# Moving the vectors' pair products from VectorE to GpSimd, and turning them by transposes that add in PSUM

## The chip, the cores and the metric

The kernel runs on one core of a Trainium2 chip. Such a core has five engines with queues of their own: TensorE (matrix products, called PE in the profile, its weight loads PEld), VectorE (DVE), ScalarE (ACT), GpSimd (POOL) and SyncE (SP), which here only starts transfers. They meet through semaphores. The metric is the time of one execution on the device in microseconds (us); lower is better.

## The reference, cut to what matters

A graph network of four layers over 6250 nodes and 206250 edges; after each layer comes `x = layernorm(x + layer(x))`. A node row has 160 numbers: 64 scalars and 32 vectors of 3 components. In the last two layers (L2 and L3) the edges' messages are summed into their node, and then the node is updated:

```python
# a0, a1: the summed messages' scalars (n, 64) and vectors (n, 32, 3); xs, xv: the node's own
u0 = jnp.einsum('nu,nv,uvw->nw', xs, a0, Wu_ss) * INV64 \
   + jnp.einsum('nui,nvi,uvw->nw', xv, a1, Wu_vv) * (INV_SQRT3 * INV32)
u1 = jnp.einsum('nu,nvi,uvw->nwi', xs, a1, Wu_sv) * INV_SQRT2048 \
   + jnp.einsum('nui,nv,uvw->nwi', xv, a0, Wu_vs) * INV_SQRT2048
u0 = u0 + xs @ Lu_s * INV8
u1 = u1 + jnp.einsum('nui,uw->nwi', xv, Lu_v) * INV_SQRT32
return node_features + jnp.concatenate([u0, u1.reshape(n, 96)], axis=-1)
```

The change concerns the second term of `u0`: for every node the 32 x 32 products of the node's vectors with the message vectors, added over the three components, and then contracted with `Wu_vv`.

## The kernel before

Each layer has an edge part (`e0` to `e3`) and a node part (`n1` to `n4`). The parts follow one another and their tiles bear the part's letter. The change lies in `nodes_update`, which is run twice, as `n3` and as `n4`. It works on 50 blocks of 128 nodes, one node to a partition. Every engine has its own instruction list, written out by hand, with a function `step(s)` that is run for every block; the lists keep their order, and semaphores alone hold them together. In one step an engine works on up to three blocks: `s` (its row is being loaded and its message sums turned), `b = s.back(1)` (its update is computed) and `p = s.back(2)` (its layer norm is finished).

- SyncE loads block `s`'s row `row`, once the update step of the block that used that buffer has been done (`upd_set`), and stores the finished block.
- GpSimd copies the message sums of block `s` out of the big accumulator into `own` (L1932), and takes the inverse root in the layer norm of block `p` (`inverse_root`, L771).
- TensorE turns rows and sums (`front`), multiplies the sums by the message weights (`messages`, which gives `agg`), and for block `b` turns the pair products in ten halves of 4 x 128 columns (`turn_half`): halves 0 to 7 are the scalars' products `ss`, halves 8 and 9 the vectors' products `vv`. ScalarE copies every turned half to SBUF, and `contract_half` contracts it with the weights `WQ`. The scalars are turned by `pe.transpose`. For the vectors, three ordinary matmuls by the identity add the three components in PSUM; an ordinary matmul of fp32 leaves two records in the trace, a transpose one. `columns` (four per block) make the matrices of which VectorE forms `u1`. Half 8 comes after `front(s)`; then contraction 7, columns 2 and 3, `messages(s)`, half 9 and contractions 8 and 9.
- VectorE forms `ss` in four pieces of 1024 and `vv` in one of 3072 elements a partition (`pair_products`, L1954 and L1959), then finishes block `p` (`finish`: the update step L1968, layer norm, L1976 as the last), and then forms the `u1` products of block `b` (`vector_products`: twice two multiplications L1988 and a sum L1993).

The piece of `ss` with number 2 or 3 reuses the buffer of number 0 or 1 and waits until TensorE has turned it. There is one `vv` buffer. `linked` counts the four linked steps of one `finish`; its last count is the memset at L1976, behind the normalisation.

Of the kernel before, what the change touches and what calls it, by code (L numbers as in the profile page):

```python
# [8 lines left out]
ALU = mybir.AluOpType  # L9
# [3 lines left out]
P = 128  # L13
# [8 lines left out]
CS, CV = 64, 32  # L22
D = CS + 3 * CV
# [66 lines left out]
def run_steps(eng, step, lag, unroll, number, held=(), peel=1):  # L90


    turns = number // unroll
    assert turns * unroll == number and lag <= unroll
    for i in range(peel):
        for j in range(unroll):
            step(Tile(i, j, unroll, number))
    with eng.Fori(peel, turns) as i:  # L98
        registers = {(a, c): eng.snap(eng.to_reg(i * a + c)) for a, c in held} or None
        for j in range(unroll):  # L100
            step(Tile(i, j, unroll, number, 0, registers))
    for j in range(lag):
        step(Tile(turns, j, unroll, number))
# [10 lines left out]
def bcast(ap, shape):  # L114
    return ap.to_broadcast(list(shape))
# [648 lines left out]
def layernorm(dve, chain, y, stats, out, squares, roots, item, nth, each):  # L764
    moments(dve, chain, y, stats, squares)
    return normalise(dve, y, stats, out, roots, item, nth, each)


def inverse_root(pool, at, power, squares, roots, item, nth, each):
    pool.wait_ge(squares, item.count(nth, each))  # L770
    pool.tensor_tensor(at, at, power, ALU.pow).then_inc(roots, 1)  # L771
# [945 lines left out]
def nodes_update(nc, g, A, name, mats, x, acc, x_out, scales, message_scales):  # L1717
# [11 lines left out]
    HALVES = 10  # L1729
    CHUNKS = 5  # L1730
    REST = CAT - 4 * P
    with Phase(nc, name) as ph:
        two = range(2)

        def pair(name, shape):
            return [ph.sb(f"{name}{k}", shape) for k in two]
        WZ, WQ, WL, WM = ph.sb("WZ", [P, 2 * CH]), ph.sb("WQ", [P, 40, CS]), ph.sb("WL", [P, 2, D]), ph.sb("WM", [P, CHUNKS, D])
        row, agg, a0T, rowT, accT, lastT = pair("row", [P, 2 * P]), pair("agg", [P, D]), pair("a0T", [P, P]), pair("rowT", [P, 2 * P]), pair("accT", [P, 4 * P]), pair("lastT", [REST, P])
        own, ss = pair("own", [P, CAT]), pair("ss", [P, SQ])
        vv = ph.sb("vv", [P, 3 * CV * CV])  # L1740
# [12 lines left out]
        row_in, stored = (ph.sems_of(n, 2) for n in ("row_in", "stored"))  # L1753

        with nc.Block() as block:
# [21 lines left out]
            def _(pe):  # L1777
# [28 lines left out]
                def turn_half(b, h):  # L1806
                    if h < 8:
                        pe.wait_ge(ss_set, b.count(h // 2 + 1, 4))
                    else:
                        pe.wait_ge(vv_set, b.count(1))  # L1810
                    if h >= 2 or b.reuses(1):
                        pe.wait_ge(half_sb, b.count(h - 1, HALVES))
                    for c in range(4):
                        to = ps_s[h % 2][:, c * P:(c + 1) * P]
                        if h < 8:
                            at = (4 * (h % 2) + c) * P
                            ins = pe.transpose(to, ss[h // 2 % 2][:, at:at + P], g.ident[:, :])  # L1817
                        else:
                            at = (4 * (h - 8) + c) * P
                            for k in range(3):  # L1820
                                ins = pe.matmul(to, vv[:, k * CV * CV + at:k * CV * CV + at + P], g.ident[:, :], start=k == 0, stop=k == 2)
                    ins.then_inc(half_ps, 1)

                def contract_half(b, h):
# [99 lines left out]
            @block.gpsimd  # L1924
            def _(pool):
                pool.wait_ge(blank, 1)

                def step(s):
                    if s.exists():
                        if s.reuses(2):  # L1930
                            pool.wait_ge(turned, s.count(-1))
                        pool.tensor_copy(own[s.j][:, :], acc[:, bass.ds(s.t() * CAT, CAT)]).then_inc(held, 1)  # L1932
                    p = s.back(2)
                    if p.exists():
                        inverse_root(pool, stats[p.j][:, 8:9], power[:, 0:1], squares, roots, p, 1, 1)
                run_steps(pool, step, 2, 2, NB)

            @block.vector
            def _(dve):
                dve.memset(power[:, :], -0.5)  # L1940
                dve.tensor_tensor(twice[:, :], g.ident[:, 0:CS], g.ident[:, CS:P], ALU.add)
                for k in two:
                    ins = dve.memset(row[k][:, D:2 * P], 0.0)
                ins.then_inc(blank, 1)
                links = Linked(dve, linked, 4)

                def pair_products(b):
                    k = b.j
                    dve.wait_ge(row_in[k], b.dma())
                    dve.wait_ge(agg_set, b.count(1))  # L1950
                    for q in range(4):
                        if q >= 2 or b.reuses(1):
                            dve.wait_ge(half_ps, b.count(2 * q - 2 if q >= 2 else 2 * q + 6 - HALVES, HALVES))
                        dve.tensor_tensor(ss[q % 2][:, :].rearrange("p (u v) -> p u v", u=16),  # L1954
                                          bcast(row[k][:, 16 * q:16 * (q + 1)].unsqueeze(2), (P, 16, CS)),
                                          bcast(agg[k][:, 0:CS].unsqueeze(1), (P, 16, CS)), ALU.mult).then_inc(ss_set, 1)
                    if b.reuses(1):
                        dve.wait_ge(half_ps, b.count(0, HALVES))
                    dve.tensor_tensor(vv[:, :].rearrange("p (c u v) -> p c u v", c=3, u=CV),  # L1959
                                      bcast(row[k][:, CS:D].rearrange("p (c u) -> p c u", c=3).unsqueeze(3), (P, 3, CV, CV)),  # L1960
                                      bcast(agg[k][:, CS:D].rearrange("p (c v) -> p c v", c=3).unsqueeze(2), (P, 3, CV, CV)),
                                      ALU.mult).then_inc(vv_set, 1)

                def finish(b):
                    k = b.j
                    links.start(b)
                    dve.wait_ge(folded, b.count(1))
                    dve.scalar_tensor_tensor(out=y[k][:, :], in0=row[k][:, 0:D], scalar=2.0, in1=ps_l[k][:, 0:D],  # L1968
                                             op0=ALU.mult, op1=ALU.add).then_inc(upd_set, 1)
                    dve.wait_ge(upd_set, b.count(1))  # L1970
                    dve.wait_ge(reduced, b.count(2, 2))
                    links.link(dve.tensor_tensor(y[k][:, CS:D], y[k][:, CS:D], sums[k][:, :], ALU.add))
                    if b.reuses(2):
                        dve.wait_ge(stored[k], b.value(16, 16 * b.off))
                    layernorm(dve, links, y[k][:, :], stats[k], new[k][:, :], squares, roots, b, 1, 1).then_inc(new_set, 1)
                    links.link(dve.memset(stats[k][:, 21:22], 0.0))  # L1976
                    links.end()

                def vector_products(b):
                    k = b.j  # L1980
                    out = prod[:, :].rearrange("p (c w t) -> p c w t", c=3, t=2 * CV)
                    for n in range(4):
                        dve.wait_ge(z_ps, b.count(n + 1, 4))
                        half, term = n // 2, n % 2
                        if half or b.reuses(1):
                            dve.wait_ge(reduced, b.count(half - 1 + 1 if half else 0, 2))
                        other = (row if term else agg)[k][:, CS:D].rearrange("p (c m) -> p c m", c=3)
                        dve.tensor_tensor(out[:, :, :, term * CV:(term + 1) * CV],  # L1988
                                          bcast(ps_z[term][:, :].rearrange("p (w m) -> p w m", w=16).unsqueeze(1), (P, 3, 16, CV)),
                                          bcast(other.unsqueeze(2), (P, 3, 16, CV)), ALU.mult).then_inc(z_used, 1)  # L1990
                        if term:
                            dve.wait_ge(z_used, b.count(n + 1, 4))
                            dve.tensor_reduce(sums[k][:, :].rearrange("p (c w) -> p c w", c=3)[:, :, 16 * half:16 * (half + 1)],  # L1993
                                              out, AX.X, ALU.add).then_inc(reduced, 1)

                def step(s):
                    b, p = s.back(1), s.back(2)
                    if b.exists():
                        pair_products(b)
                    if p.exists():  # L2000
                        finish(p)
                    if b.exists():
                        vector_products(b)
                run_steps(dve, step, 2, 2, NB)
# [176 lines left out]
```

## Time and profile before

| | us |
|---|---|
| median of 3 runs | 20541.54 (20539.68 to 20549.04) |
| profiled execution | 20573.62 |
| its span | 20572.0 |
| TensorE busy | 17578.1 (85%) |
| VectorE busy | 16081.1 (78%) |
| ScalarE busy | 12429.6 (60%) |
| GpSimd busy | 12351.1 (60%) |

The span runs from the first to the last instruction of the profiled execution. Busy times are sums over the whole program; n3 and n4 take roughly 15626 to 16975 and 19224 to 20572 us of it, and in them the engines stand quite differently from the whole: GpSimd, at 60% overall, is nearly idle there. In a timeline a row is a run of like instructions of one engine: start, duration, engine, line, operation, output <- inputs, count, and in brackets how long the engine stood idle before it and which instruction released it. With several instructions in a row, the duration goes from the first start to the last end; the ends of TensorE's matmuls are modelled.

### The profile page before, as it was taken

How to read it: one execution, taken by the hardware profiler on the slowest of the kernel's cores; microseconds unless marked ns; L12 is line 12 of the kernel's file. 1: busy time of each engine (PE TensorE's matmuls, PEld its weight loads, DVE VectorE, ACT ScalarE, POOL GpSimd, SP SyncE). 2: the span in 40 equal slices, each digit the busy share in tenths (PEclk: the TensorE clock that was granted, in tenths of full speed). 3: DMA queues.
4: the chain of work that ended last, by engine and by line, in shares of the span. 5: the costliest groups of instructions: out<-in, count | busy, mean ns of one | idle time of the engine just before them, and what ended most of it. 6: DMA issues, size and time to landing. Idle time of an engine off the chain costs nothing. (4 is left out here: it accounts for less than half of the span.)

```text
span 20572.0 us, 465117 instructions
## 1 busy us (share of the span) xinstructions
PE 17578.1 (85%) x121874; PEld 14135.8 (69%) x121874; DVE 16081.1 (78%) x44638; ACT 12429.6 (60%) x39738; POOL 12351.1 (60%) x13048
## 2 busy tenths in 40 slices
PE   2777666676699999999999999699998889999888
PEld 1333322222588888888888888699997669999766
DVE  3777799998588888888988888655556885555688
ACT  1222288887277777777777777267774226777422
POOL 2777777776367666666767676177772007777200
PEclk8888789888899999999999999999999999999999
DMA  2666577777744444444444444522222002222200
GB/s 83 170 171 171 164 136 142 140 141 127 240 121 123 122 121 122 122 121 122 124 123 123 122 121 122 140 64 67 67 67 30 6 6 63 67 67 67 30 6 6
DMA packets 1922898, 2132.27 MB, mean 104 GB/s; under 512 B 745584, under 2 KB 1597712, under 8 KB 1922544
## 3 DMA queue, kind: packets, MB, share of 16 engines
q0 software_dynamic: 567456, 1314.26, 24.1%
q1 hardware_dynamic: 1355344, 816.91, 16.1%
q8 instruction: 36, 0.59, 0.0%
q14 instruction: 62, 0.51, 0.0%
HBM read 1518.49 MB, written 611.44 MB: 104 GB/s over the span
## 5 line engine op out<-in xcount | busy, mean ns | idle before, releaser
L1639 POOL DMA_INDIRECT e_rows<-x,e_take x3456 | 3335.2, 965 | 1143.1 <-issue 1056.8
L1673 ACT ACTIVATE e_hot<-e_hot,e_here 128x128 f32<-128x128 f32 x10368 | 3123.5, 387 | 1389.2 <-DVE e_hot L1696 1381.3
L1659 PE MATMUL e_sums<-e_rows,e_hot 128*128 128x128 f32 x20736 | 2878.9, 275 | 0.0
L1659 PEld LDWEIGHTS e_sums<-e_rows,e_hot 128*128 128x128 f32 x20736 | 2678.9, 192 | 0.0
L632 PE MATMUL e_sums<-e_feat,e_same 128*128 128x480 f32 x3456 | 1761.3, 661 | 858.0 <-DVE e_feat L712 385.3
L615 POOL DMA_INDIRECT e_rows<-table,e_take x1728 | 1925.8, 1114 | 649.1 <-issue 620.9
L1214 ACT ACTIVATE e_m<-e_th,e_yt 128x64 f32<-128x64 f32 x6480 | 2301.3, 426 | 0.0
L1076 POOL DMA_INDIRECT e_srow<-src_table,e_at x1620 | 1615.2, 997 | 926.0 <-issue 917.8
L1087 POOL DMA_INDIRECT comb<-e_crow,e_at x1620 | 1664.6, 1028 | 823.7 <-issue 524.9
L771 POOL TENSOR_TENSOR n_stats<-n_stats,n_power 128x1 f32<-128x1 f32 x250 | 145.4, 582 | 3153.5 <-DVE n_stats L756 3066.4
L632 PEld LDWEIGHTS e_sums<-e_feat,e_same 128*128 128x128 f32 x3456 | 721.1, 219 | 1898.2 <-issue 1416.3
L1079 POOL DMA_INDIRECT e_crow<-comb,e_at x1620 | 1673.0, 1033 | 493.7 <-issue 449.2
L327 POOL DMA_INDIRECT pay_rows<-order_stage,order_put x1620 | 1582.3, 977 | 498.2 <-issue 370.2
L1120 PE MATMUL e_ps_m<-ident,e_m 128*128 128x128 f32 x12960 | 1808.6, 284 | 25.5 <-DVE e_m L1352 8.0
L1655 PE MATMUL e_sums<-e_rows,e_hot 128*128 128x160 f32 x6912 | 1580.1, 310 | 196.1 <-DMA e_rows<-x,e_take 111.7
L1696 DVE TENSOR_TENSOR e_hot<-e_iota,e_here 128x512 f32<-128x512 f32 x864 | 599.3, 694 | 1282.1 <-PE e_sums L1659 1282.1
L1120 PEld LDWEIGHTS e_ps_m<-ident,e_m 128*128 128x128 f32 x12960 | 1504.9, 150 | 84.4 <-DVE e_m L1352 10.0
L1656 PE MATMUL e_sums<-e_rows,e_hot 128*128 128x160 f32 x6912 | 1506.6, 300 | 0.0
L421 ACT ACTIVATE order_stage<-order_ps_w 128x448 f32<-128x448 f32 x810 | 441.8, 545 | 1505.8 <-PE order_ps_w L389 1502.6
L1145 PE MATMUL e_ps_h<-e_WV,e_m2T 128*128 128x32 f32 x9720 | 1317.9, 273 | 0.0
L658 ACT ACTIVATE e_feat<-e_feat,e_pay 128x64 f32<-128x64 f32 x5184 | 1280.7, 333 | 54.0 <-DVE e_feat L687 45.5
L1707 DVE TENSOR_TENSOR acc<-acc,e_sums 128x320 f32 x1728 | 843.3, 488 | 540.4 <-issue 289.1
(331 smaller groups left out, 46900.9 us busy)
## 6 DMA issues: line engine op xcount, KB each, us to landing
e_pay<-pay_rows SPq DMA_DIRECT2D x432, 470.0 KB
order_keys<-key_row SPq DMA_DIRECT2D x810, 128.0 KB
e_keys<-key_row SPq DMA_DIRECT2D x810, 128.0 KB, 3.4
comb<-n_comb SPq DMA_DIRECT2D x600, 164.0 KB, 2.0
e_rows<-x,e_take POOLq DMA_INDIRECT x3456
order_feat<-in_attr_T SPq DMA_DIRECT2D x810, 64.0 KB
e_basis<-in_attr_T SPq DMA_DIRECT2D x1620, 32.0 KB
e_comps<-in_attr_T SPq DMA_DIRECT2D x1620, 32.0 KB
```

What stands on the lines that cost most here:

```text
L327: pool.indirect_dma_start(out=pay_rows, out_offset=bass.IndirectOffsetOnAxis(ap=put[t.j // 2][:, 2 * (t.j % 2) + q:2 * (t.j % 2) + q + 1], ...
L615: pool.indirect_dma_start(out=rows[t.j][:, q, 0:D], out_offset=None, in_=table, in_offset=bass.IndirectOffsetOnAxis(ap=take[t.j][:, q:q + ...
L632: ins = pe.matmul(sums[b][q // G][:, 0:AGG0], same[b][:, q, :], feat[b][:, q, 0:AGG0], start=q % G == 0, stop=q % G == G - 1)
L1076: pool.indirect_dma_start(out=srow[n.j % 3][:, q, :], out_offset=None, in_=src_table, in_offset=bass.IndirectOffsetOnAxis(ap=at[n.j][:, q: ...
L1079: pool.indirect_dma_start(out=crow[n.j][:, q, 0:COMB], out_offset=None, in_=combs[2 * n.j + q][0:NP, :], in_offset=bass.IndirectOffsetOnAx ...
L1087: pool.indirect_dma_start(out=combs[2 * w.j + q], out_offset=bass.IndirectOffsetOnAxis(ap=at[w.j][:, 4 + q:5 + q], axis=0), in_=crow[w.j][ ...
L1120: ins = pe.transpose(ps_m[q][:, c * P:(c + 1) * P], m[n.j % 2][:, q, c * P:(c + 1) * P], g.ident[:, :])
L1214: ins = act.activation(m2[k][:, q, c * P:c * P + CS], th[k][:, q, 0:CS], ACT.Identity, scale=y, bias=y)
L1639: pool.indirect_dma_start(out=rows[t.j][:, q, 0:D], out_offset=None, in_=x, in_offset=bass.IndirectOffsetOnAxis(ap=take[t.j][:, q:q + 1], ...
L1655: pe.matmul(to[:, 0:D], one[:, q, 0, :], row[:, q, 0:D], start=first, stop=last)
L1659: ins = pe.matmul(bass.AP(o.tensor, o.offset, [o.ap[0], [DOT - CS * c, 2], [1, CS]]), one[:, q, 2 + c, :], bass.AP(r.tensor, r.offset, [r. ...
L1673: ins = act.activation(one[:, q, 2 + c, :], one[:, q, 0, :], ACT.Copy, scale=here[t.j][:, q, TOWARDS + c:TOWARDS + c + 1])
```

## The change

VectorE's `pair_products` no longer forms `vv`. GpSimd does: in step `s`, behind its root for block `p`, it waits until all four linked steps of `p`'s `finish` are done, then for block `b`'s row, for `agg`, and until the ten halves of the block before have been turned, and issues the same multiplication. In the first step with a block `b` there is no `p` yet and the first of these waits is missing. On TensorE the three matmuls by the identity become three transposes that add in PSUM.

```diff
                         else:
                             at = (4 * (h - 8) + c) * P
                             for k in range(3):
-                                ins = pe.matmul(to, vv[:, k * CV * CV + at:k * CV * CV + at + P], g.ident[:, :], start=k == 0, stop=k == 2)
+                                ins = pe.matmul(to, vv[:, k * CV * CV + at:k * CV * CV + at + P], g.ident[:, :], is_transpose=True,
+                                                start=k == 0, stop=k == 2)
...
                     p = s.back(2)
                     if p.exists():
                         inverse_root(pool, stats[p.j][:, 8:9], power[:, 0:1], squares, roots, p, 1, 1)
+                        pool.wait_ge(linked, p.count(4, 4))
+                    b = s.back(1)
+                    if b.exists():
+                        k = b.j
+                        pool.wait_ge(row_in[k], b.dma())
+                        pool.wait_ge(agg_set, b.count(1))
+                        if b.reuses(1):
+                            pool.wait_ge(half_ps, b.count(0, HALVES))
+                        pool.tensor_tensor(vv[:, :].rearrange("p (c u v) -> p c u v", c=3, u=CV),
+                                           bcast(row[k][:, CS:D].rearrange("p (c u) -> p c u", c=3).unsqueeze(3), (P, 3, CV, CV)),
+                                           bcast(agg[k][:, CS:D].rearrange("p (c v) -> p c v", c=3).unsqueeze(2), (P, 3, CV, CV)),
+                                           ALU.mult).then_inc(vv_set, 1)
                 run_steps(pool, step, 2, 2, NB)
...
-                    if b.reuses(1):
-                        dve.wait_ge(half_ps, b.count(0, HALVES))
-                    dve.tensor_tensor(vv[:, :].rearrange("p (c u v) -> p c u v", c=3, u=CV),
-                                      bcast(row[k][:, CS:D].rearrange("p (c u) -> p c u", c=3).unsqueeze(3), (P, 3, CV, CV)),
-                                      bcast(agg[k][:, CS:D].rearrange("p (c v) -> p c v", c=3).unsqueeze(2), (P, 3, CV, CV)),
-                                      ALU.mult).then_inc(vv_set, 1)
```

In VectorE's list, in the second of the two steps of the loop body of n3, these rows stood one behind another (line, operation, output <- inputs, shape):

```order
L1954 TENSOR_TENSOR n_ss<-n_row,n_agg 128x1024
L1959 TENSOR_TENSOR n_vv<-n_row,n_agg 128x3072
L1968 SCALAR_TENSOR_TENSOR n_y<-n_row,n_ps_l 128x160
L1972 TENSOR_TENSOR n_y<-n_y,n_sums 128x96
L753 BN_STATS n_stats<-n_y 128x6
```

The same place now (the new lines push the line numbers up by 13, then 7):

```order
L1967 TENSOR_TENSOR n_ss<-n_row,n_agg 128x1024
L1975 SCALAR_TENSOR_TENSOR n_y<-n_row,n_ps_l 128x160
L1979 TENSOR_TENSOR n_y<-n_y,n_sums 128x96
L753 BN_STATS n_stats<-n_y 128x6
L754 MEMSET n_stats 128x1
```

The update step of the older block follows the last scalar products directly.

In GpSimd's list the loop body of n3 was, from its branch to the loop's end (ISA and register rows carry the waits and the loop's counting):

```order
L98 UNCONDITIONAL_BRANCH
L98 ISA
L1932 ISA
L1932 COPY n_own<-acc 128x544
L771 TENSOR_TENSOR n_stats<-n_stats,n_power 128x1
L1932 ISA
L1932 COPY n_own<-acc 128x544
L771 TENSOR_TENSOR n_stats<-n_stats,n_power 128x1
```

And now, from the first step's copy on:

```order
L1933 COPY n_own<-acc 128x544
L771 TENSOR_TENSOR n_stats<-n_stats,n_power 128x1
L1937 ISA
L1941 REGISTER_ALU
L1944 ISA
L1945 TENSOR_TENSOR n_vv<-n_row,n_agg 128x3072
L1933 ISA
L1933 COPY n_own<-acc 128x544
L771 TENSOR_TENSOR n_stats<-n_stats,n_power 128x1
L1941 REGISTER_ALU
L1945 TENSOR_TENSOR n_vv<-n_row,n_agg 128x3072
```

The products stand between the root of one block and the copy of the next, so the copy, which came right behind the root, now comes behind the products. TensorE's list keeps its order.

## Rows read from the trace of the kernel before

**Rows 1.** Stretches of n2 and n4: length; busy PE, PEld, DVE, ACT, POOL; clock; DMA.
```profile
13136.00:13140.00 4.00, 4.00 (x15) 4.00 (x16) 2.15 (x13) 0.00 (x0) 0.55 (x1) 0.50 0.64 166
...
19310.00:20500.00 1190.00, 1063.77 (x9154) 804.03 (x9151) 1062.26 (x868) 353.00 (x729) 52.38 (x92) 1.00 0.02 6
```

**Rows 2.** Timeline of VectorE, one block of n4.
```profile
20017.29 3.70 DVE L1954 TENSOR_TENSOR n_ss<-n_row,n_agg 128x1024 f32<-128x1024 f32 x3
20022.51 1.23 DVE L1954 TENSOR_TENSOR n_ss<-n_row,n_agg 128x1024 f32<-128x1024 f32 x1 [1.52 <-PE n_ps_s L1817]
20023.66 3.35 DVE L1959 TENSOR_TENSOR n_vv<-n_row,n_agg 128x3072 f32<-128x3072 f32 x1
20026.93 0.31 DVE L1968 SCALAR_TENSOR_TENSOR n_y<-n_row,n_ps_l 128x160 f32<-128x160 f32 x1
...
20029.15 0.65 DVE L761 TENSOR_SCALAR n_new<-n_y,n_stats 128x160 f32<-128x160 f32 x1 [0.67 <-POOL n_stats L771]
20029.75 0.06 DVE L1976 MEMSET n_stats<- 128x1 f32 x1
20030.02 1.76 DVE L1988 TENSOR_TENSOR n_prod<-n_ps_z,n_agg 128x1536 f32<-128x1536 f32 x1 [0.21 <-DVE n_stats L1976]
...
20036.86 1.76 DVE L1988 TENSOR_TENSOR n_prod<-n_ps_z,n_agg 128x1536 f32<-128x1536 f32 x1
...
20043.59 1.22 DVE L1954 TENSOR_TENSOR n_ss<-n_row,n_agg 128x1024 f32<-128x1024 f32 x1
```

**Rows 3.** Timeline of TensorE in the same block.
```profile
20029.19 0.44 PE L1788 MATMUL n_ps_t<-ident,n_row 128*128 128x128 f32 x2 [1.43 <-DMA n_row<-x]
...
20030.01 2.84 PE L1821 MATMUL n_ps_s<-ident,n_vv 128*128 128x128 f32 x24
...
20033.90 0.59 PE L1841 MATMUL n_ps_z<-n_WZ,n_rowT 64*128 64x512 f32 x1
...
20034.55 1.35 PE L1801 MATMUL n_ps_a<-n_WM,n_accT 128*128 128x160 f32 x8
...
20042.95 0.81 PE L1853 MATMUL n_ps_l<-n_WL,n_rowT 128*128 128x160 f32 x4
20044.86 1.09 PE L1817 MATMUL n_ps_s<-ident,n_ss 128*128 128x128 f32 x8 [1.10 <-DVE n_ss L1954]
```

**Rows 4.** Timeline of GpSimd in the same block.
```profile
20029.06 0.64 POOL L1932 COPY n_own<-acc 128x544 f32 x1
```

**Rows 5.** Timeline of VectorE, the last layer norms of n3.
```profile
16946.49 0.31 DVE L1968 SCALAR_TENSOR_TENSOR n_y<-n_row,n_ps_l 128x160 f32<-128x160 f32 x1
...
16948.84 0.06 DVE L1976 MEMSET n_stats<- 128x1 f32 x1
```

**Rows 6.** Groups of GpSimd by form: count, busy us, mean ns, idle before.
```profile
L1932 POOL COPY n_own<-acc 128x544 f32 x96 | 61.2, 638 | 44.5 <-PE n_ps_a L1792 44.5
L926 POOL COPY n_agg<-acc 128x480 f32 x46 | 27.4, 595 | 0.1
...
L310 POOL IOTA order_gran_i<- 128x864 int32 x1 | 0.9, 853 | 0.0
L1631 POOL IOTA e_iota_i<- 128x128 int32 x2 | 0.5, 240 | 10.7 <-POOLq L131 10.7
```

**Rows 7.** Timeline of TensorE in n2.
```profile
13126.03 3.61 PE L1477 MATMUL n_ps_m<-n_runs,ident 128*128 128x164 f32 x24 [1.63 <-DVE n_runs L1540]
...
13136.00 6.47 PE L1477 MATMUL n_ps_m<-n_runs,ident 128*128 128x164 f32 x24 [4.86 <-DVE n_runs L1540]
...
13281.71 5.28 PE L1477 MATMUL n_ps_m<-n_runs,ident 128*128 128x164 f32 x24 [3.84 <-DVE n_runs L1540]
```

**Rows 8.** Timeline of VectorE and GpSimd in n1.
```profile
5399.10 1.01 DVE L977 TENSOR_TENSOR n_nrm<-n_nrm,n_gam 128x160 f32<-128x160 f32 x1
5399.33 0.59 POOL L926 COPY n_agg<-acc 128x480 f32 x1
...
5407.06 0.33 DVE L977 TENSOR_TENSOR n_nrm<-n_nrm,n_gam 128x160 f32<-128x160 f32 x1
```

## Prediction

> **What bounds the kernel now.** The change touches only the last two node parts (n3 and n4, one function). I read the table of stretches first: in a settled stretch of n4 TensorE and VectorE are each busy 89% of the time, GpSimd 4%, at a granted clock of 1.00, which is the 2.4 GHz level [rows 1]. Two engines that are nearly full can still wait for each other, so I then laid VectorE's and TensorE's timelines over one block side by side [rows 2, 3]. A block begins with VectorE's first scalar product `n_ss` at 20017.29, and the next one begins at 20043.59; over the part the distance from block to block is 26.1 us.
>
> In that block VectorE waits in three places: 1.52 us before the fourth `n_ss`, because TensorE must first have turned earlier ones, 0.67 us for GpSimd's root, and 0.21 us before the products [rows 2]. TensorE waits 1.43 us for the `n_row` transfer and 1.10 us for the first `n_ss` [rows 3]. So VectorE's chain sets the period, and `n_vv` (3.35 us) lies on it: layer norm, products and the next block's `n_ss` are queued behind it.
>
> **What goes.** Without `n_vv`, the older block's first update step moves from 20026.93 to the place of `n_vv`, 6.37 us after the block's start (20023.66 - 20017.29) [rows 2]. VectorE alone would then need 26.1 - 3.3 = 22.8 us. A second saving comes with it: today `n_own`'s copy on GpSimd lies on top of the normalisation, which takes 0.65 us [rows 2, 4]; in the last block, which has no such copy, the closing memset ends 2.41 us after the update step began (16948.84 + 0.06 - 16946.49), against 2.88 us in the settled block [rows 2, 5]. After the change the copy stands behind the pair products, so I take 2.41 us.
>
> TensorE's pieces: 24 records of `n_vv` per half take 2.84 us, so their starts lie (2.84 - 0.27)/23 = 0.11 us apart [rows 3]. Eight transposes take 1.09 us, 0.12 us apart, with one record each [rows 3]. Twelve transposes instead of twenty-four records save 12 x 0.11 = 1.3 us per half, 2.7 us per block. If an adding transpose needed two records too, nothing would be saved; if it were slower than the plain ones, something could be lost, and I leave 1.3 us per half for that in the range.
>
> **What comes.** GpSimd's multiplication is the unknown: no row shows a wide two-input operation on that engine. The nearest below is the same instruction on VectorE, 3.35 us [rows 2]. From GpSimd's own rows: copies of 480 and 544 elements take 595 and 638 ns, that is 0.67 ns for each further element and 0.27 us at the start; making and writing one costs 0.84 ns (an iota of 864 in 853 ns, of 128 in 240 ns) [rows 6]. If two operands are read one after the other and a result is made, 2 x 0.67 + 0.84 = 2.18 ns x 3072 + 0.27 us = 7.0 us. Above lie three streams at the copy's whole rate of 1.17 ns, 10.8 us. I take 7.0 us, since it rests on the engine's own rows.
>
> The Trainium skill, page "GPSIMD Engine Reference", section 3.1, has 4497 ns for a two-input add of 2048 fp32 elements, about twice VectorE; scaled to 3072 that is an estimate of 6.7 us, by which the loop below would be 0.3 us shorter and the forecast 29 us lower. As a rule it speaks against the move.
>
> **The new loop.** The products start on GpSimd only when the older block's layer norm has ended, and TensorE's half 8 waits for them. Queued behind that wait on TensorE are contraction 7, columns 2 and 3 (which VectorE's second half of the products needs), the messages and half 9. The loop is therefore: 6.37 us to the update step; 2.41 us to its end; 0.15 us to GpSimd's start; 7.0 us; then TensorE from half 8 to the end of the columns, 20034.49 - 20030.01 = 4.48 us today (33.90 + 0.59), less 1.34, plus 0.2 for the signals, 3.3 us [rows 3]; then VectorE's second half until the next block, 20043.59 - 20036.86 = 6.73 us [rows 2]. Sum: 26.0 us, against 26.1 us now. The first half of the products (6.84 us, 30.02 to 36.86) lies under GpSimd's 7.0 us, and VectorE then stands idle for 3.6 us. TensorE's own way back is no later: from the messages at 34.55 to `n_WL` at 42.95 it needs 8.40 - 1.34 = 7.06 us and some 0.7 us for `n_WL`, and the next `n_ss` is ready 8.1 us after the same point [rows 2, 3]. So everything that VectorE gives up comes back as a wait, and the steady period alone would hardly change.
>
> **The clock.** The wait is new for TensorE. The row transfer starts 3.3 us earlier, so the 1.43 us wait in front of `n_ps_t` goes and the transposes there end 11.3 us after the block's start (29.19 - 1.43 + 0.82 - 17.29) [rows 2, 3]. Half 8 begins at 6.37 + 2.41 + 0.15 + 7.0 + 0.15 = 16.1 us: 4.8 us without work in each block. In an earlier part TensorE had such waits: after one of 4.86 us the granted clock was 0.50, the 1.2 GHz level, and a group of 24 matmuls took 6.47 us where it takes 3.61 us otherwise; after 3.84 us the same group took 5.28 us [rows 1, 7]. The loss was 1.7 to 2.9 us for 3.6 us of work. Here 3.1 us of work stand between the wait and VectorE's next start, and the messages behind have only 0.3 us to spare, so I count 1.5 us of it: 27.5 us a block, 1.4 us more.
>
> **Sum.** Two parts have 98 distances from block to block, the first of each without a layer norm; 96 x 1.4 = 134 us. At each part's start there is no older block, so GpSimd's products lie beside the first `n_ss`, and both read two operands from SBUF. A two-input VectorE instruction took 1.01 us instead of 0.33 us when a GpSimd copy ran beside it [rows 8]: they don't share. That makes VectorE's first chain later by 7.0 - 3.35 = 3.6 us, twice, 8 us in all. At the ends the columns wait today for VectorE anyway, and I count nothing. Together +142 us on the profiled execution's 20573.62 us; that lies 32 us above the median of the three runs, 20541.54 us, and the forecast stands on the median: 20541.5 + 142 = 20684, say 20685 us.
>
> **Rivals.**
> 1. *GpSimd is quick.* If writing hides under reading, two streams at 0.67 ns make 4.4 us. The loop is 23.4 us, TensorE's wait only 2.5 us, and the clock may hold as it does today after 1.43 us. 96 x (26.1 - 23.4) = 260 us less: 20285 us. The copy's slope speaks for it, the iota's against. Faster from about 5.6 us of GpSimd time down if the clock falls as counted (19.0 + 1.5 + 5.6 = 26.1).
> 2. *The clock holds.* The loop stays at 26.0 us: 20535 to 20550 us, no change. Every wait over 3.8 us in rows 7 speaks against it.
> 3. *The products that VectorE forms meanwhile are held up too.* They read one operand from PSUM and one from SBUF. If they can't run beside GpSimd, all 13.57 us of them (30.02 to 43.59) come after it: 6.37 + 2.41 + 0.15 + 7.0 + 13.6 = 29.5 us, 96 x 3.4 + 8 = 334 us more, 20875 us. Rows 8 show the conflict for two SBUF operands, and the one-tensor normalisation suffered as well (0.65 us); no row shows an operation fed from PSUM under a GpSimd copy. The Trainium skill, page "SBUF — State Buffer", section on the ports, says that VectorE with at most one SBUF input and outside its two-port modes does not contend; by that rule this rival falls away.
> 4. *GpSimd is slow*, 8 us or more: 19.0 + 8 + 1.5 = 28.5 us, 96 x 2.4 = 230 us, 20780 us and up; 10.8 us would give 21050 us.
>
> **Chances.** Forecast (5.8 to 7.8 us with a lowered clock) 56%; rival 1 18%; rival 2 12%; rival 3 7%; rival 4 7%. The range 20430 to 20900 us leaves out most of rival 1 and the upper end of rival 4, some 20%. The forecast's own range, with the two-record bound and 1.0 to 2.0 us for the clock, is 20560 to 20800 us. A change under 0.2% (41 us) can't be told from none here. Faster by more: rival 1 and a little of the forecast's lower edge, 20%; within: rival 2 and the forecast's edge, 15%; slower: 65%.
>
> **What would show it.** In the changed profile: `n_vv` on GpSimd at 7.0 us, starting 0.1 to 0.2 us after the memset that ends the layer norm; the normalisation well under 0.65 us; 12 records per half, 1.4 to 1.6 us at the 2.4 GHz level; a wait of about 5 us before `n_ps_s` from `n_vv` on TensorE and about 4 us before the third product on VectorE; a granted clock below 1.00 in the settled stretch; 27.5 us between blocks. The forecast is wrong if `n_vv` takes under 5.6 us, if the clock stays at 1.00, or if the products grow beyond 1.76 us.

## The result, and the profile after

The changed kernel takes 20573.9 us (median of 20 runs, 20558.17 to 20607.74); the kernel before took 20539.97 us in 20 runs beside it. The ratio is 1.002, interval 1.0013 to 1.0027: slower by 34 us, where the prediction said slower by 142 us.

The table of stretches has this row for the settled stretch of n4 (columns as in [rows 1]):

```profile
19310.00:20500.00 1190.00, 1021.86 (x7889) 721.03 (x7890) 883.15 (x799) 343.37 (x711) 287.77 (x134) 0.90 0.02 6
```

VectorE fell from 89% busy to 74% (883.15 of 1190), GpSimd rose from 4% to 24%, and the granted clock fell from 1.00 to 0.90. VectorE has less to do and the part is longer all the same: what it gave up came back as waiting. One block of n4 in VectorE's timeline shows where (it answers to [rows 2]):

```profile
20017.84 3.63 DVE L1967 TENSOR_TENSOR n_ss<-n_row,n_agg 128x1024 f32<-128x1024 f32 x3
20022.91 1.23 DVE L1967 TENSOR_TENSOR n_ss<-n_row,n_agg 128x1024 f32<-128x1024 f32 x1 [1.44 <-PE n_ps_s L1817]
20024.06 0.31 DVE L1975 SCALAR_TENSOR_TENSOR n_y<-n_row,n_ps_l 128x160 f32<-128x160 f32 x1
...
20026.10 0.36 DVE L761 TENSOR_SCALAR n_new<-n_y,n_stats 128x160 f32<-128x160 f32 x1 [0.67 <-POOL n_stats L771]
20026.41 0.06 DVE L1983 MEMSET n_stats<- 128x1 f32 x1
20026.67 1.76 DVE L1995 TENSOR_TENSOR n_prod<-n_ps_z,n_agg 128x1536 f32<-128x1536 f32 x1 [0.21 <-DVE n_stats L1983]
...
20036.75 1.76 DVE L1995 TENSOR_TENSOR n_prod<-n_ps_z,n_agg 128x1536 f32<-128x1536 f32 x1 [3.26 <-PE n_ps_z L1842]
...
20043.47 3.70 DVE L1967 TENSOR_TENSOR n_ss<-n_row,n_agg 128x1024 f32<-128x1024 f32 x3
```

The update step (L1975) stands at the place of the old `n_vv`, 6.2 us after the block's start; the normalisation takes 0.36 us instead of 0.65; the products keep their 1.76 us. New is the wait of 3.26 us before the third product, for TensorE's columns (4.73 us in the block before). GpSimd in the same block, and the group of `n_vv` over both parts (ns: shortest, median, longest):

```profile
20026.73 5.37 POOL L1945 TENSOR_TENSOR n_vv<-n_row,n_agg 128x3072 f32<-128x3072 f32 x1 [0.67 <-DVE n_stats L1983]
...
L1945 POOL TENSOR_TENSOR n_vv<-n_row,n_agg x100: 5360/5368/6403, 15640.4 to 20582.8; 128x3072 f32<-128x3072 f32 x100
```

`n_vv` starts 0.26 us after the memset ended and takes 5.37 us, not 7.0. TensorE in the block before, in that block and, as the last row, two blocks later (it answers to [rows 3]):

```profile
20005.12 2.82 PE L1821 MATMUL n_ps_s<-ident,n_vv 128*128 128x128 f32 x12 [3.33 <-POOL n_vv L1945]
20007.87 1.12 PE L1829 MATMUL n_ps_l<-n_turnedT,n_WQ 128*64 128x128 f32 x8
...
20014.08 1.53 PE L1821 MATMUL n_ps_s<-ident,n_vv 128*128 128x128 f32 x12
...
20032.16 2.82 PE L1821 MATMUL n_ps_s<-ident,n_vv 128*128 128x128 f32 x12 [3.09 <-POOL n_vv L1945]
20034.91 0.66 PE L1829 MATMUL n_ps_l<-n_turnedT,n_WQ 128*64 128x128 f32 x8
...
20084.09 1.53 PE L1821 MATMUL n_ps_s<-ident,n_vv 128*128 128x128 f32 x12 [3.09 <-POOL n_vv L1945]
```

A half of `n_vv` has 12 records now: 1.53 us behind steady work (20014.08), 2.82 us behind the first two waits of 3.1 to 3.3 us, and 1.53 us again behind the last one. The stretches say why (wait, work behind it, and the same again; then the work behind the last wait; the clock is the third column from the end):

```profile
20001.80:20005.10 3.30, 0.00 (x0) 0.00 (x0) 3.27 (x2) 1.01 (x3) 3.30 (x2) 0.86 0.00 0
20005.10:20010.90 5.80, 5.78 (x24) 3.65 (x24) 1.29 (x1) 0.60 (x1) 0.54 (x1) 0.50 0.00 0
20029.00:20032.10 3.10, 0.07 (x1) 0.00 (x0) 3.07 (x2) 1.01 (x3) 3.10 (x2) 0.90 0.00 0
20032.10:20035.00 2.90, 2.84 (x14) 2.51 (x16) 1.39 (x1) 0.00 (x0) 0.59 (x2) 0.52 0.00 0
20084.10:20087.00 2.90, 2.90 (x24) 2.00 (x24) 1.32 (x1) 0.60 (x1) 0.52 (x1) 1.00 0.00 0
```

Around the end of most such waits the clock falls to the 1.2 GHz level. In the first block the columns are slow too, in the second only the turned half, and in the last the clock holds at 1.00. Of the 96 settled blocks of n3 and n4, 57 are like the first (27.2 us from block to block on the mean), 33 have a shorter low stretch (26.0 us), and in 6 the clock holds (24.5 us).

From the first update step to the 49th, the mean distance from block to block is 26.64 us in n3 and 26.61 us in n4, against 26.14 and 26.12 us before. From the first `n_ss` to the last update step, n3 takes 1332.5 us against 1305.6 and n4 1329.8 against 1305.1: 51.6 us more, 96 x 0.5 = 48 of it settled blocks. The rest of this profiled run was 17.6 us shorter, nearly all of it ahead of n3, where nothing differs: n3's start lies anywhere from 15622.58 to 15679.14 us in the thirteen profiled runs told of here.

### The profile page after: what moved, and what is told of

The parts are those of the page before. It is cut to its first block and busy times, and to the rows that moved or that the text cites. A ratio compares the mean times of both kernels' runs of the same rounds, so it can differ in the third digit from the quotient of the medians.

```text
span 20606.1 us, 460565 instructions
## 1 busy us (share of the span) xinstructions
PE 17536.0 (85%) x119474; PEld 13976.2 (68%) x119474; DVE 15727.7 (76%) x44538; ACT 12433.1 (60%) x39738; POOL 12910.4 (63%) x13148
## 5 line engine op out<-in xcount | busy, mean ns | idle before, releaser
L771 POOL TENSOR_TENSOR n_stats<-n_stats,n_power 128x1 f32<-128x1 f32 x250 | 145.5, 582 | 2577.3 <-DVE n_stats L756 2490.2
L1914 ACT ACTIVATE n_turnedT<-n_ps_s 128x512 f32<-128x512 f32 x1000 | 586.7, 597 | 1208.0 <-PE n_ps_s L1817 643.4
```

## Experiments

"Distance" is the mean from block to block in n4, taken as above. A ratio is to the kernel before, run on the same chip. The three runs with full operands have one time each and are read by their profile.

**1. The transposes alone** (before, with the change's first hunk only).

```diff
-ins = pe.matmul(to, vv[...], g.ident[:, :], start=k == 0, stop=k == 2)
+ins = pe.matmul(to, vv[...], g.ident[:, :], is_transpose=True, start=k == 0, stop=k == 2)
```

> The kernel before with the transposes alone: VectorE still forms the pair products. Theory (VectorE's chain sets the period before the change): TensorE gains 1.3 us per half, but what it gains becomes waiting: in front of the first scalar products 2.4 us instead of 1.1 us, and for the columns. The settled distance between blocks stays at 26.1 us, the time within 0.2% of before (20540 us). Rival (TensorE counts too): 1 to 2.7 us per block less, 96 to 260 us faster.

Measured: 20738.32 us against 20625.03, ratio 1.0055 (1.0042 to 1.0069), distance 27.54 us. A miss. TensorE and VectorE in one block of n4, and the wait with the work behind it:

```profile
20042.40 1.96 PE L1817 MATMUL n_ps_s<-ident,n_ss 128*128 128x128 f32 x8 [2.50 <-DVE n_ss L1955]
```
```profile
20044.40 1.22 DVE L1955 TENSOR_TENSOR n_ss<-n_row,n_agg 128x1024 f32<-128x1024 f32 x1 [1.00 <-PE n_ps_s L1817]
20047.44 1.23 DVE L1955 TENSOR_TENSOR n_ss<-n_row,n_agg 128x1024 f32<-128x1024 f32 x1 [1.82 <-PE n_ps_s L1817]
```
```profile
20039.90:20042.40 2.50, 0.00 (x1) 0.01 (x1) 2.50 (x3) 0.00 (x0) 0.00 (x0) 0.92 0.00 0
20042.40:20045.40 3.00, 3.00 (x18) 2.81 (x18) 2.00 (x2) 1.19 (x2) 0.00 (x0) 0.50 0.00 0
```

TensorE is done earlier and waits 2.50 us for `n_ss`, where it waited 1.10 us [rows 3]. The clock is low behind that wait, the turning of `n_ss` takes 1.96 us instead of 1.09, and VectorE, which needs it for its later `n_ss`, waits 1.00 and 1.82 us, 1.3 us more than its 1.52 before [rows 2]. Less work on TensorE cost 1.4 us a block; three of the 48 blocks, with a longer low stretch, take 28.87 us.

**2. GpSimd alone** (the changed kernel, with matmuls against the identity as before).

```diff
-ins = pe.matmul(to, vv[...], g.ident[:, :], is_transpose=True, start=k == 0, stop=k == 2)
+ins = pe.matmul(to, vv[...], g.ident[:, :], start=k == 0, stop=k == 2)
```

> The changed kernel without the transposes: GpSimd forms the products, TensorE turns them by the old matmuls. Theory (a loop over GpSimd's products and TensorE's half 8, plus a lowered clock behind TensorE's wait): half 8 stands in the loop, so the loop is 1.3 us longer than after, 26.0 us at 2.4 GHz and 27.5 to 28.5 us with the lowered clock; 130 to 220 us slower than before. Rival (the transposes bring nothing, or themselves lower the clock): as after, 26.6 us, or faster than after.

Measured: 20875.31 us against 20625.03, ratio 1.0123 (1.0107 to 1.0138), distance 28.97 us: the direction as expected, some more than the upper end. TensorE, then VectorE, in n4:

```profile
20107.81 4.57 PE L1821 MATMUL n_ps_s<-ident,n_vv 128*128 128x128 f32 x24 [3.33 <-POOL n_vv L1944]
...
20117.08 2.94 PE L1821 MATMUL n_ps_s<-ident,n_vv 128*128 128x128 f32 x24
```
```profile
20124.08 1.23 DVE L1966 TENSOR_TENSOR n_ss<-n_row,n_agg 128x1024 f32<-128x1024 f32 x1 [0.86 <-PE n_ps_s L1817]
```

The wait and the lowered clock are there as with the transposes. What the expectation lacked is the second half: with 24 records TensorE comes late to the next block's `n_ss`, and VectorE waits 0.86 us before its third one too. The single settled block of n4 in which the clock held (update step at 19463.1) took 26.83 us, against the 26.0 expected at 2.4 GHz. Here the transposes are worth 2.4 us a block (28.97 - 26.61); alone they cost 1.4.

**3. The wait filled with products that nobody reads.**

```diff
-else:
-    pe.wait_ge(vv_set, b.count(1))
 if h >= 2 or b.reuses(1):
     pe.wait_ge(half_sb, b.count(h - 1, HALVES))
+if h == 8:
+    for _ in range(12):
+        pe.matmul(ps_s[0][:, 0:P], g.ident[:, :], g.ident[:, :], start=True, stop=True)
+if h >= 8:
+    pe.wait_ge(vv_set, b.count(1))
```

> The changed kernel with 12 identity matmuls in front of TensorE's wait for the products, written to the half's own PSUM region and overwritten by it. Theory (the lowered clock behind the wait costs 1.9 us of the 26.6 us a block): granted clock 1.00 in the settled stretch, half 8 at 1.5 us in every block, every distance near 24.7 us as the shortest ones after, 170 to 190 us faster than after and 110 to 150 us faster than before (20390 to 20430 us). Rival (the loop itself is 26.6 us, the clock is not what costs): no change from after, or slower by the matmuls.

Measured: 20459.63 us against 20625.03, ratio 0.992 (0.9907 to 0.9934), distance 24.53 us: as expected, the gain a little larger. TensorE in n4, and the settled stretch:

```profile
20001.51 2.84 PE L1813 MATMUL n_ps_s<-ident 128*128 128x128 f32 x24
20004.76 1.53 PE L1824 MATMUL n_ps_s<-ident,n_vv 128*128 128x128 f32 x12 [0.41 <-POOL n_vv L1948]
```
```profile
19310.00:20400.00 1090.00, 1040.24 (x8943) 778.15 (x8937) 878.56 (x803) 343.82 (x712) 291.78 (x134) 1.00 0.02 7
```

TensorE does more work in the same order, the clock stays at 1.00, the half takes 1.53 us. The lowered clock therefore costs 26.61 - 24.53 = 2.1 us of a block on the mean, more than the whole loss against the kernel before. The changed kernel itself agrees: its 6 blocks in which the clock held took 24.5 us.

**4. The order on TensorE changed:** contraction 7, columns 2 and 3 and the messages ahead of the first `n_vv` half; ScalarE copies the messages one half sooner.

```diff
-if h < HALVES - 1:
+if h < HALVES - 1 and h != 7:
...
+                                turn_half(b, h + 1)
...
-if h == 8 and s.exists():
+if h == 7 and s.exists():
```

> The changed kernel with contraction 7, columns 2 and 3 and the messages in front of half 8 on TensorE, and ScalarE's copies of the messages in front of its copy of half 8. Theory (GpSimd's 5.4 us cost only because the columns and messages are queued behind the wait for them): the products are ready before half 8 begins, VectorE's own chain sets the period again, 22.8 to 23.2 us a block, no wait over 2 us on TensorE, granted clock 1.00; 280 to 320 us faster than before, 20220 to 20260 us. Rival (GpSimd's products hold up VectorE's, or the clock falls in another place): over 24.5 us a block.

Measured: 20274.12 us against 20625.03, ratio 0.9832 (0.9819 to 0.9845), distance 22.56 us. VectorE, then TensorE, in n4:

```profile
20030.72 3.35 DVE L2001 TENSOR_REDUCE n_sums<-n_prod 128x48 f32<-128x3072 f32 x1
20034.10 1.76 DVE L1996 TENSOR_TENSOR n_prod<-n_ps_z,n_agg 128x1536 f32<-128x1536 f32 x1
```
```profile
20034.91 2.84 PE L1821 MATMUL n_ps_s<-ident,n_vv 128*128 128x128 f32 x24
...
20042.17 1.09 PE L1817 MATMUL n_ps_s<-ident,n_ss 128*128 128x128 f32 x8 [1.19 <-DVE n_ss L1968]
```

The third product follows the reduction without a wait, both halves come in 2.84 us without one, TensorE's longest wait in a settled block is 1.2 us, and the clock falls in none of them. This version beats both kernels, the one before by 1.7% (351 us, more than the 280 to 320 expected): VectorE now needs about what it was said to need alone (22.8 us).

**5. GpSimd without its wait for the layer norm.**

```diff
-pool.wait_ge(linked, p.count(4, 4))
```

> The changed kernel without GpSimd's wait for the older block's layer norm, so that its pair products may begin as soon as the row is in and the older products have been turned. Theory (two operands from SBUF on both engines don't run side by side): the pair products fall beside the next block's scalar products, as they do in the first block of each part, where n_vv takes 6.40 us instead of 5.36 us and three n_ss take 9.10 us instead of 3.70 us. VectorE's chain then carries some 5.4 us more than the 22.8 us that it needs alone: about 28 us from block to block, against 26.6 us in the changed kernel, and a time some 100 to 160 us above the changed kernel's. Rival (the wait for the layer norm is what costs, and the products would find room earlier): the products end earlier, TensorE's wait before n_vv and the lowered clock go, and the distance is 22.8 to 24 us, 250 us or more below the kernel before.

Measured: 20792.89 us against 20563.49, ratio 1.0115 (1.0099 to 1.0132), distance 28.4 us. The distance is as expected; the time lies 229 us above the kernel before, some 195 above the changed one, where 100 to 160 were expected; and the place is another. GpSimd, then VectorE, in n4:

```profile
20011.38 0.55 POOL L771 TENSOR_TENSOR n_stats<-n_stats,n_power 128x1 f32<-128x1 f32 x1 [21.30 <-DVE n_stats L756]
20011.90 5.36 POOL L1944 TENSOR_TENSOR n_vv<-n_row,n_agg 128x3072 f32<-128x3072 f32 x1
```
```profile
20003.38 3.70 DVE L1966 TENSOR_TENSOR n_ss<-n_row,n_agg 128x1024 f32<-128x1024 f32 x3
...
20011.97 5.39 DVE L761 TENSOR_SCALAR n_new<-n_y,n_stats 128x160 f32<-128x160 f32 x1 [0.67 <-POOL n_stats L771]
```

The older block's root (L771) stands ahead of the products in GpSimd's queue, so they start right behind it and not beside `n_ss`, which keep their 3.70 us. The normalisation, 0.07 us later, takes 5.39 us instead of 0.36: it ends with GpSimd's product. GpSimd's wait for the layer norm, 0.67 us in the changed kernel, is what keeps the product from standing there.

**6. The wait filled with transposes** (as 3, with 24 transposes of the identity).

```diff
...
+if h == 8:
+    for _ in range(24):
+        pe.transpose(ps_s[0][:, 0:P], g.ident[:, :], g.ident[:, :])
...
```

> The changed kernel with 24 transposes of the identity (about 24 x 0.12 = 2.9 us) put into TensorE's wait before the turning of the pair products, where the earlier run had 12 fp32 products of the same size in 24 records; their results are never read. Theory A (any work in the wait holds the clock): as with the products, a low clock for under 2% of the settled stretch and 24.5 us from block to block, 0.6 to 0.9% under the kernel before. Theory B (transposes don't keep the clock up; the Trainium skill, page 'TensorE: Matmul & The Clock Gate', Part 4, says that a transpose does not count as PE-busy in the same way): the clock falls as in the changed kernel, 15 to 20% of the stretch at the lower level, and 26 to 27 us from block to block.

Measured: 20412.84 us against 20563.49, ratio 0.9925 (0.9909 to 0.9942), distance 24.54 us. TensorE and the settled stretch of n4:

```profile
20018.81 2.79 PE L1813 MATMUL n_ps_s<-ident 128*128 128x128 f32 x24
20022.07 1.53 PE L1824 MATMUL n_ps_s<-ident,n_vv 128*128 128x128 f32 x12 [0.47 <-POOL n_vv L1948]
```
```profile
19310.00:20400.00 1090.00, 1032.80 (x8891) 769.01 (x8891) 879.44 (x797) 340.53 (x704) 286.18 (x132) 1.00 0.02 7
```

Transposes held the clock as well as products did: theory A. The Trainium skill's page "TensorE: Matmul & The Clock Gate", Part 4, says that the full clock does not engage for transpose mode, which does not count as busy in the same way; in this kernel the measurement (1.00) decides against it, as far as holding the clock goes. Whether transposes alone would raise it, no run here shows. In experiment 1, too, it was most likely the longer wait and not the kind of work behind which the clock fell: in experiment 4 the same transposes ran with the clock up.

**7, 8 and 9. Full operands on GpSimd:** both, only the first (the row, in which each number is read 32 times in a row), only the second (runs of 32 numbers, read 32 times over). The diff is that of the first; each of the others replaces one operand.

```diff
-bcast(row[k][:, CS:D]...unsqueeze(3), (P, 3, CV, CV)),
-bcast(agg[k][:, CS:D]...unsqueeze(2), (P, 3, CV, CV)),
+acc[:, 0:3 * CV * CV]...,
+acc[:, 3 * CV * CV:6 * CV * CV]...,
```

> The changed kernel, with GpSimd's multiplication reading two full tensors of 3072 elements side by side (parts of the accumulator) in place of the two short operands that are each read again and again; the pair products are then not those of the reference. Theory A (repeating a short operand is as dear as reading a long one): n_vv stays at 5.36 us, 1.75 ns for each element. Theory B (the short operands are cheap, and full ones go at the rate of the Trainium skill, page 'GPSIMD Engine Reference', section 3.1, that is 4497 ns for 2048 or an estimate of 6.7 us for 3072): n_vv takes 6.5 to 7 us, and the distance from block to block grows by as much, to about 28 us.

> The changed kernel with only GpSimd's first operand (the own row, in which every number is read 32 times in a row) replaced by a full tensor of 3072 elements; the pair products are not those of the reference. Theory A (the number that is read again and again in a row is what is cheap): n_vv takes about 6.7 us, as with two full operands. Theory B (the short run of 32 numbers that is read again is what is cheap): it stays at 5.4 us. Theory C (each of the two saves a part): about 6.0 us.

> The changed kernel with only GpSimd's second operand (the gathered vectors, in runs of 32 numbers that are read 32 times over) replaced by a full tensor of 3072 elements; the pair products are not those of the reference. Theory A: n_vv stays at 5.4 us. Theory B: about 6.7 us. Theory C: about 6.0 us.

Measured: 20688.58, 20662.67 and 20592.39 us; distances 27.31, 27.36 and 26.66 us. The group of `n_vv` in each of the three, in that order:

```profile
L1945 POOL TENSOR_TENSOR n_vv<-acc x100: 6697/6706/7711, 15642.9 to 20662.1; 128x3072 f32<-128x3072 f32 x100
```
```profile
L1945 POOL TENSOR_TENSOR n_vv<-acc,n_agg x100: 6689/6706/7707, 15622.6 to 20636.2; 128x3072 f32<-128x3072 f32 x100
```
```profile
L1945 POOL TENSOR_TENSOR n_vv<-n_row,acc x100: 5363/5371/6404, 15626.4 to 20567.3; 128x3072 f32<-128x3072 f32 x100
```

Two full operands take 6.71 us, and so does the full row alone; with the full second operand it stays at 5.37: theories B, A and A. What makes GpSimd quicker here than with full operands is the operand that stands still for 32 elements, and it alone. The distance did not grow by as much as the product, as theory B of the first run had it, but by 0.7 us. That run also shows the clock's share at a longer product. TensorE in n4 of it:

```profile
20014.05 2.82 PE L1821 MATMUL n_ps_s<-ident,n_vv 128*128 128x128 f32 x12 [4.67 <-POOL n_vv L1945]
20016.80 0.74 PE L1829 MATMUL n_ps_l<-n_turnedT,n_WQ 128*64 128x128 f32 x8
```

Its distance is 27.33 us (mean of both parts); without a clock loss it would by estimate be 24.53 + (6.71 - 5.37) = 25.87, so the clock costs some 1.5 us there.

**10. The kernel before, reordered** (the diff of 4 on the kernel before).

> The kernel before, its pair products still on VectorE and turned by matmuls, with only the order of the reordered run: contraction 7, columns 2 and 3 and the messages ahead of the first n_vv half on TensorE, and ScalarE's copies of the messages one half earlier. Theory: VectorE's own chain sets the period before (22.8 us and 3.3 us of n_vv), so the order alone gives nothing: 26.1 us from block to block, within 0.3% of the kernel before, or slower, if TensorE's waits for n_ss grow and the clock falls behind them. Rival: the order is what made the reordered run faster, with or without GpSimd, and this kernel too is more than 1% faster.

Measured: 20796.43 us against 20563.49, ratio 1.0114 (1.0097 to 1.0131), distance 28.54 us: slower, as the theory allowed, and not faster as the rival had it. In n4 most distances are 27.5 us, and about one in six is 33.2. One such, in VectorE's timeline, with TensorE's slow stretch in it:

```profile
20008.86 1.23 DVE L1955 TENSOR_TENSOR n_ss<-n_row,n_agg 128x1024 f32<-128x1024 f32 x1 [7.08 <-PE n_ps_s L1817]
```
```profile
19987.90:20001.50 13.60, 13.60 (x44) 9.49 (x44) 13.50 (x7) 0.57 (x2) 0.00 (x0) 0.50 0.00 0
```

TensorE, then VectorE, in the next block, a usual one:

```profile
20020.67 1.12 PE L1841 MATMUL n_ps_z<-n_WZ,n_rowT 64*128 64x512 f32 x2 [0.81 <-DVE n_prod L1989]
...
20026.50 5.63 PE L1821 MATMUL n_ps_s<-ident,n_vv 128*128 128x128 f32 x48
```
```profile
20036.28 1.23 DVE L1955 TENSOR_TENSOR n_ss<-n_row,n_agg 128x1024 f32<-128x1024 f32 x1 [1.50 <-PE n_ps_s L1817]
```

The order alone is no gain: with `n_vv` on VectorE the products begin late, columns 2 and 3 wait for them, and the two `n_vv` halves pile up behind, ahead of the next `n_ss`, for whose turning VectorE then waits 1.50 us more. The gain of 4 needs GpSimd and the order together. The long blocks are those in which the clock lies at 0.50 for much of the block. TensorE's waits ahead of that stretch, 1.54 and 0.96 us, are hardly longer than those of the usual block behind it (1.52 and 0.81 us), so what lets the clock fall in some blocks and not in others stays open.

**11. The reordered kernel with the old matmuls** (the diff of 2 on that of 4).

> The reordered kernel (pair products on GpSimd, columns and messages ahead of the first n_vv half on TensorE), with the old matmuls against the identity in place of the transposes. Theory: in the reordered kernel TensorE stands still for only 1.2 us in each block (before the first n_ss); twice 24 records instead of twice 12 cost 2 x 1.3 = 2.6 us, so some 1.5 us come through to the turning of the next n_ss, for which VectorE's later n_ss wait: about 24 us from block to block instead of 22.56, clock still up, 0.9 to 1.1% under the kernel before. Rival (the transposes matter little once the order is right): 22.6 us and 1.7% under it.

Measured: 20339.51 us against 20552.3, ratio 0.9893 (0.9876 to 0.9909), distance 23.94 us. TensorE, then VectorE, in n4:

```profile
20019.14 5.62 PE L1821 MATMUL n_ps_s<-ident,n_vv 128*128 128x128 f32 x48
...
20027.84 1.04 PE L1817 MATMUL n_ps_s<-ident,n_ss 128*128 128x128 f32 x8
```
```profile
20028.92 1.23 DVE L1967 TENSOR_TENSOR n_ss<-n_row,n_agg 128x1024 f32<-128x1024 f32 x1 [1.50 <-PE n_ps_s L1817]
```

As expected: the halves take 5.62 us instead of 2.84, TensorE has no wait left before `n_ss` and VectorE waits 1.50 us more. In the right order the transposes are worth 1.4 us a block.

## Why the prediction was right in direction and wrong in size

**The step that failed is the price of GpSimd's multiplication.** It stood at 7.0 us, two operands read one after the other at the copy's slope and one result written. Measured are 5.37 us, inside the bounds of 3.35 and 10.8, below the forecast's own 5.8 to 7.8. For two full operands the working was near (6.71 us in experiment 7); it did not weigh that one operand stands still for 32 elements, which saves 1.34 of the 1.63 us. The estimate from the Trainium skill's page "GPSIMD Engine Reference", section 3.1, 6.7 us, agrees with the full operands (6.71 us) and missed for the same reason. With 6.71 us on GpSimd the kernel takes 110 and 125 us more than the one before on the same chip (one time each), where 142 us more were forecast for 7.0.

**That the direction was right is in part luck.** With 5.37 us in the prediction's own sum a block takes 19.0 + 5.37 + 1.5 = 25.9 us, less than the 26.1 before, and by its own sign (`n_vv` under 5.6 us) the forecast was wrong. That the changed kernel is slower all the same comes from the clock, which cost 0.6 us a block more than was counted.

**The clock** was put at 1.5 us a block. At 6.71 us on GpSimd it is by estimate 1.5; at the real 5.37 us it is 2.1 (26.61 - 24.53). The shorter wait did not make it cheaper: in 57 of 96 blocks the low stretch now goes on through the columns (5.80 us of work at 0.50 at 20005.10), where with 6.71 us it ends with the turned half in 94 of 96. A quicker GpSimd thus gained only 0.7 us of its 1.34. Why the low stretch is longer, shorter or absent behind waits of the same length is not shown. That the clock would fall behind the new wait, as in [rows 7], was right in most blocks, and experiments 3 and 6 show it by taking the wait's idleness away.

**The loop** without the clock was said to be 19.0 us and GpSimd's time. With 5.37 us that makes 24.37; the filled wait gives 24.53. The update step's move, the normalisation (0.36 us), GpSimd's start (0.26 instead of 0.15 us) and the columns' way are as they were put, to 0.2 us in all.

**The transposes** save 1.3 us per half as worked out (2.84 to 1.53 us). The prediction let them count in full in one half and not at all in the other; experiment 2 against the changed kernel says 2.4 us for both with the lowered clock in play, experiment 11 against 4 says 1.4 us. That alone they would cost something (experiment 1) it did not ask, and the expectation had it wrong.

**The first blocks** were put at +8 us. VectorE and GpSimd in the first block of n3:

```profile
15640.36 9.10 DVE L1967 TENSOR_TENSOR n_ss<-n_row,n_agg 128x1024 f32<-128x1024 f32 x3 [31.35 <-ACT n_a0T L1902]
15640.41 6.40 POOL L1945 TENSOR_TENSOR n_vv<-n_row,n_agg 128x3072 f32<-128x3072 f32 x1 [30.11 <-ACT n_a0T L1902]
```

Three `n_ss` beside `n_vv` took 9.10 us instead of 3.70 and `n_vv` itself 6.40 instead of 5.37, so the conflict was there. But the next block's `n_ss` came only 1.5 us later than before (26.84 us after the first one, against 25.32), since `n_vv` and a wait of 2.24 us left VectorE's chain. The parts' ends together came to 51.6 - 48 = +4 us.

**Sum by the measured terms:** per block 1.4 us were forecast; GpSimd -1.63, the clock +0.6, the rest of the loop +0.16 make 0.5, and 96 x 0.5 + 4 = 52 us, which is what the two parts show. Over whole runs the medians differ by 34 us, and the ratio's interval reaches from 27 to 55 us. Two slips in the working move the forecast by no more than 3 us: the iotas' slope is 0.83 ns and not 0.84, and TensorE's wait under rival 1 comes to 2.2 us by the prediction's own terms (13.5 - 11.3), not 2.5.

**The rivals.** Rival 1 (quick GpSimd) had the point at which the sign turns at about 5.6 us; at 5.37 us the kernel is still slower, because the clock costs 2.1 and not 1.5 us: 19.16 + 2.1 leaves 4.9 us for an even loop, if the clock's price stays. Rival 2 (the clock holds) falls with 0.90. Rival 3 (products held up) falls: fed from PSUM they took 1.76 us under `n_vv` (20026.67 beside 20026.73), as the Trainium skill's page "SBUF — State Buffer", section "Who interferes with whom", has it for VectorE with one SBUF input at most and outside its two-port modes. Rival 4 falls with 5.37 us.

## What to carry to other kernels

Work that is moved to an idle but slower engine can come back as waiting in its consumer's queue, so look at that queue's order too: the same move lost 0.2% with other work queued behind the waiting instruction and gained 1.7% with that work ahead of it. With the old order and the wait merely filled it gained 0.8%. A wait on TensorE is to be priced with the slow work behind it (here 2.1 us a block on the mean for 3.1 to 3.3 us of waiting), and a saving on TensorE that only lengthens such a wait can cost time. Before a two-input operation goes to GpSimd, look which operand stands still, and keep it from running beside VectorE's operations between SBUF tensors.

## What the runs showed of the hardware that was not expected

- GpSimd's multiplication of 128x3072 fp32 took 5.37 us with a first operand that repeats each number 32 times in a row, 6.71 us with a full one; the second operand's repeated runs saved nothing (5.37 with it full).
- A small VectorE operation on SBUF tensors that started 0.07 us behind GpSimd's product took 5.39 us instead of 0.36, and ended 0.1 us after it; one fed from PSUM and SBUF kept its 1.76 us under such a product.
- Transposes that add in PSUM have one record each: 12 took 1.53 us where 24 records of matmuls took 2.84. Filled into a wait, transposes kept the granted clock at 1.00, as products did.
- The clock was at 0.50 behind TensorE waits of 2.50 us (experiment 1) and behind most of 3.09 to 3.33 us (the changed kernel), but held at 1.00 in 6 of the 96 blocks there. Behind 1.43 us [rows 3] the work had its usual length; in about one block in six of n4 in experiment 10 the clock fell all the same, behind waits of 1.54 and 0.96 us.
